# Attention row scores on 64 rows of the TensorE array, two heads at once, in bursts of four, with four PSUM banks instead of three

## What is computed

```python
q, k, v = (proj(Wq), proj(Wk), proj(Wv))            # 16 heads of 16
scores = jnp.einsum('bhsd,bhtd->bhst', q, k) * scale
scores = jnp.where(mask[None, None, :, :], -jnp.inf, scores)
attn = jax.nn.softmax(scores, axis=-1)
out = jnp.einsum('bhst,bhtd->bhsd', attn, v)        # then Wo, rms norm, modulation
x = x + ...                                          # then a top-2-of-8 expert block,
                                                     # a low-rank block and a quaternion block
```

## Time and profile before

| | |
|---|---|
| median of 3 runs | 1164.3 us (1163.31 to 1166.56) |
| span of the profiled execution | 1162.1 us |
| PE busy | 1122.4 us, 97% |
| DVE busy | 770.8 us, 66% |
| ACT busy | 803.1 us, 69% |
| POOL busy | 512.6 us, 44% |

### The profile page before, as it was taken

How to read it: one execution, slowest core, us unless ns; L and a number is a source line. 1 busy time by engine, 2 the same in 40 slices (tenths; PEclk the granted TensorE clock), 3 DMA queues, 4 the chain that set the end, 5 groups by cost and what they waited for, 6 DMA issues and landing times.

```text
span 1162.1 us, 23399 instructions
## 1 busy us (share of the span) xinstructions
PE 1122.4 (97%) x7520; PEld 763.4 (66%) x7520; DVE 770.8 (66%) x2265; ACT 803.1 (69%) x1752; POOL 512.6 (44%) x837
## 2 busy tenths in 40 slices
PE   8899999999999999998989999999999999999988
PEld 4333434434334343342418999998999999999968
DVE  4877777787887878878745434355555555667747
ACT  2578888787787877877786756655666666666645
POOL 8424135583755837657462365354222223222220
PEclk8999999999999999999999999999999999999999
DMA  8665638367384572843837488856566766723536
GB/s 220 193 195 189 219 100 250 124 215 231 119 257 138 198 235 94 242 157 133 286 101 269 115 309 306 267 120 133 155 193 190 213 193 179 226 48 70 164 91 217
DMA packets 101616, 213.64 MB, mean 184 GB/s; under 512 B 10917, under 2 KB 71341, under 8 KB 93046
## 3 DMA queue, kind: packets, MB, share of 16 engines
q1 hardware_dynamic: 86038, 192.42, 51.1%
q0 software_dynamic: 14304, 18.69, 9.0%
q10 hardware_dynamic: 1152, 1.05, 0.4%
HBM read 239.28 MB, written 74.29 MB: 270 GB/s over the span
## 4 chain that ended last, share of the span: by engine, by line
PE 46%; ACT 3%; issue 1%; DVE 1%; POOL 1%; DMA 1%; another core or an unknown queue 0%; ACTq 0%; POOLq 0%
PE bank L1084 38%; PE bank L1247 1%; PE bank L1189 1%; PE bank L1099 1%; ACT pt L1355 1%; PE bank L1170 1%; DMA x<-yout,rows 1%; PE bank L1113 1%; PE bank L1174 1%; PE bank L1207 1%; PE bank L1282 0%; PE bank L1155 0%; PE bank L1227 0%; ACT full L1433 0%
## 5 line engine op out<-in xcount | busy, mean ns | idle before, releaser
L1628 DVE CUSTOM_DVE_ANT_0 junk<-bank,mneg 128x512 bf16<-128x512 f32 x512 | 333.0, 683 | 119.0 <-PE bank L1155 116.3
L1355 ACT ACTIVATE pt<-bank 128x512 f32<-128x512 f32 x512 | 301.0, 594 | 67.8 <-PE bank L1170 29.7
L1975 POOL DMA_INDIRECT x<-yout,rows x78 | 122.8, 1574 | 292.9 <-ACT yout L1438 249.6
L1084 PE MATMUL bank<-hid,w 128*128 128x256 f32 x1872 | 242.7, 286 | 4.2 <-DVE hid L1776 3.8
L1084 PEld LDWEIGHTS bank<-hid,w 128*128 128x128 f32 x1872 | 229.3, 190 | 6.0 <-issue 4.8
L1776 DVE TENSOR_TENSOR hid<-full,hid 128x256 fp32r<-128x256 f32 x312 | 133.3, 431 | 135.3 <-ACT full L1433 126.8
L1428 ACT ACTIVATE hid<-bank,biases 128x256 fp32r<-128x256 f32 x312 | 149.4, 479 | 91.6 <-PE bank L1084 88.0
L1433 ACT ACTIVATE full<-bank,biases 128x256 f32<-128x256 f32 x312 | 148.7, 477 | 0.0
L1174 PE MATMUL bank<-mneg,identb 128*128 128x512 bf16 x386 | 146.9, 381 | 0.0
L1084 PE MATMUL bank<-rowsT,w 128*128 128x256 f32 x936 | 122.9, 284 | 0.9 <-issue 0.9
L1084 PE MATMUL bank<-w,hid 128*128 128x256 f32 x936 | 121.9, 283 | 1.5 <-DVE hid L1776 1.5
(11 more groups left out here) (184 smaller groups left out, 1445.2 us busy)
## 6 DMA issues: line engine op xcount, KB each, us to landing
w<-split_weights SPq DMA_DIRECT2D x80, 1024.0 KB
w<-split_weights SPq DMA_DIRECT2D x40, 2048.0 KB
split_weights<-w_parts SPq DMA_DIRECT2D x64, 512.0 KB, 3.8
w_parts<-in_W SPq DMA_DIRECT2D x64, 256.0 KB, 4.3
split_parts<-parts SPq DMA_DIRECT2D x28, 384.0 KB, 2.6
rows<-routed SPq DMA_DIRECT2D x39, 258.0 KB, 3.4
stacks<-split_parts SPq DMA_DIRECT2D x36, 256.0 KB, 5.2
qst<-split_parts SPq DMA_DIRECT2D x24, 256.0 KB, 5.3
```

Source lines behind the costliest of these rows:

```text
L1084: product = T.matmul(ps, w[p], x[q], start=(k == 0 and n == 0), stop=(k == len(weights) - 1 and n == 2))
L1355: A.activation(pt[n % len(pt)][:, :], bank[3 + n % 2][:, :], ACT.Exp, scale=float(D) ** -0.5).then_inc(exped.sem, 1)
L1628: V.tensor_tensor_reduce(junk[n % 2][:, :], bank[n % 3][:, :], mneg[:, 0, st, :], 1.0, FLOOR, ALU.add, ALU.max, rowmax[gi % 2][:, hh, st:s ...
L1975: G.indirect_dma_start(x2_dram, bass.IndirectOffsetOnAxis(ap=rows[j % NS][:, tt, E + 1:E + 2].bitcast(U32), axis=0), yout[j % NY][:, tt], ...
```

## The change

- The row scores take four pairs of parts (64 contraction rows) instead of six (96). The stacks are laid out anew: heads 0 and 1 of each group have these 64 rows at partitions 0 to 63, heads 2 and 3 at partitions 64 to 127. The products of a step's four rows are issued together, at the step's start, in the order heads 0, 2, 1, 3, so that neighbours lie on different halves of the array. DVE still reads them one by one.
- The rows have four banks (0, 1, 2, 7). As long as there are rows, all side work and `maxima_rows` use bank 6 alone. Steps of the chain that need it are put off until one of certain steps or two columns stand between them and the last user, and the places at which `todo` is worked off change.
- `weigh` comes after the second column of its step instead of the third; `maxima_rows` at the end of a group's first step instead of its second.
- The columns of heads 2 and 3 use all 128 rows (some of them zero), those of heads 0 and 1 the same 98.
- The stacks are filled by 24 transfers in a batch, of half the size, and the shift rows by two instead of one. POOL writes the constants of the shift as fp32 words and zeroes the unused rows.
- In the first two groups the rows go one by one: first heads 0 and 1 of both groups, then heads 2 and 3. The projections of the next batch come one step earlier.

```diff
+ROW_PAIRS = 4
+KR = ROW_PAIRS * D
+ROW_HEADS = (0, 2, 1, 3)
+ROW_BANKS = (0, 1, 2, 7)
...
-FIRST_PROJECTS = range(3, 7)
+FIRST_PROJECTS = range(2, 6)
...
+ONE_BANK = ("project", "project_v", "modulation", "maxima_rows", "project_o", "turn_x1", "gate", "place")
+APART = 2
...
+def slot_of(h):
+
+    g, hh = divmod(h, GH)
+    return hh // 2 * (H // 2) + g * (GH // 2) + hh % 2
+
+
+def pair_rows(half, r):
+
+    if r < ROW_PAIRS:
+        first, step = half * KR + r, ROW_PAIRS
+    else:
+        first, step = (KR, KR // 2)[half] + r - ROW_PAIRS, len(PAIRS) - ROW_PAIRS
+    return slice(first, first + (D - 1) * step + 1, step)
...
+def bank_free(order):
+
+    cols = 0
+    for step in reversed(order):
+        if step[0] in ONE_BANK:
+            return False
+        if step[0] in ("layer1", "layer2", "layer3"):
+            return True
+        cols += step[0] == "col"
+        if cols == APART:
+            return True
+    return True
...
+            if 2 <= i < GROUPS:
+                out.append(("rows", i, k))
             for n in range(GH):
-                if i < GROUPS:
-                    out.append(("row", i, n, k))
-                if k == 0 and n == 0 and 0 <= i - 1 < GROUPS:
+                if i < 2:
+                    found = first_rows[(i * ST + k) * GH + n]
+                    out.extend((("one_row", *found), ("row", *found)))
+                elif i < GROUPS:
+                    out.append(("row", i, ROW_HEADS[n], k))
...
-                if n == 2 and k % 2 == 0 and 0 <= g < GROUPS:
+                if n == 1 and k % 2 == 0 and 0 <= g < GROUPS:
                     out.append(("weigh", g, kt))
                     out.append(("weigh", g, kt + 1))
...
+                if n == 1 and k % 2 and i >= 2 and todo and todo[0][0] != "project" and bank_read(out.order):
+                    work_off()
...
-            for _ in range(2 if len(todo) > 12 else 1):
-                if todo and i >= 2:
-                    work_off()
+            if todo and i >= 2 and (k or i > GROUPS) and bank_read(out.order):
+                work_off()
...
+        home = 6 if row_steps[0] < turn_place[s] < row_steps[-1] else 6 + n % 2
...
                     for r in range(n, len(PAIRS), STACK_STEPS):
-                        start((qst, kst)[qk][b % 2][r:KQ:len(PAIRS), :, :].rearrange("d (a h) s -> d a (h s)", a=2),
-                              split_dram[b, qk, PAIRS[r][qk]].rearrange("(a d h) s -> d a (h s)", a=2, d=D)).then_inc(dma_stack[qk], 16)
+                        for half in range(2):
+                            start((qst, kst)[qk][b % 2][pair_rows(half, r), half * (H // 2):(half + 1) * (H // 2), :],
+                                  split_dram[b, qk, PAIRS[r][qk]][half * P:(half + 1) * P, :].rearrange("(d h) s -> d h s", d=D)
+                                  ).then_inc(dma_stack[qk], 16)
...
+        def row_product(gi, hh, st):
+            b, half, at_slot = gi // NG, hh // 2, slot_of(gi % NG * GH + hh)
+            n = row_place[gi, hh, st]
+            if n >= len(ROW_BANKS):
+                pe.wait_ge(*max_found.at(rows_at[n - len(ROW_BANKS)]))
+            elif ROW_BANKS[n] == 7:
+                pe.wait_ge(*evicted(before_rows_user))
+            stacks_loaded(pe, b, half)
+            rows = slice(half * KR, (half + 1) * KR)
+            T.matmul(bank[ROW_BANKS[n % len(ROW_BANKS)]][:, :], qst[b % 2][rows, at_slot, st * P:(st + 1) * P],
+                     kst[b % 2][rows, at_slot, :], start=True, stop=True).then_inc(row_scored.sem, 1)
...
+        def shift_constants(i):
+
+            halves = [slice(half * (H // 2), (half + 1) * (H // 2)) for half in range(2)]
+            for stacks in (kst, qst):
+                constant(G.memset, stacks[i][0:KR // 2, halves[1], :].bitcast(F32), 0.0)
+            for half in range(2):
+                constant(G.memset, kst[i][shift_rows_of(half), halves[half], :].bitcast(F32), TWO_MINUS_ONES)
```

More of the change, by code:

```diff
@@ L1 @@
+import struct
 import numpy as np
@@ L123, in wait_ge, with shift_rows_of, bank_read, chain @@
             self.engine.wait_ge(sem, value)
-def chain(b, out):
+def slot_of(h):
[7 more added lines that the diff above has]
+    return slice(first, first + (D - 1) * step + 1, step)
+def shift_rows_of(half):
+    return slice(0, SHIFTS) if half else slice(KQ, KQ + SHIFTS)
+def bank_free(order):
[9 more added lines that the diff above has]
+    return True
+def bank_read(order):
+    last = next(step[0] for step in reversed(order) if step[0] in ONE_BANK + ("logits", "ranks"))
+    return last not in ("gate", "place")
+def chain(b, out, attention=False):
+    def bank():
+        while attention and not bank_free(out.order):
+            yield
     apart = 2 if b == B - 1 else 1
@@ L148, in chain @@
         yield
+        yield from bank()
         out.append(("turn_x1", b, k))
@@ L265, in work_off @@
         if step[0] == "chain":
-            chains.append(chain(step[1], out))
+            chains.append(chain(step[1], out, True))
         else:
@@ L270, in work_off @@
                 rests.append(("rest",) + step[1:])
-        if todo and todo[0][0] == "stack":
+        if todo and todo[0][0] in ("stack", "chain"):
             work_off()
@@ L287, in attention_order @@
     out.extend(value_steps(0))
+    first_rows = [(i, hh, st) for n in range(2) for i in range(2) for st in range(ST) for hh in (2 * n, 2 * n + 1)]
     for i in range(GROUPS + 3):
@@ L771, in misc_bank @@
     def misc_bank(step):
-        n = misc_place[step]
-        return bank[6 + n % 2], n >= 2 and evicted(misc_users[n - 2])
+        home, user = misc_home[step]
+        if home == 7 and user == before_rows_user and turn_place[step] > row_steps[-1]:
+            return bank[home], max_found.at(rows_at[-1])
+        return bank[home], user and evicted(user)
     def value_bank(b, st):
@@ L1147, in tensor_program @@
                 T.matmul(ps[0:B, :], condS[:, :], wc, start=True, stop=True).then_inc(modulated.sem, 1)
-            elif name == "row":
-                gi, hh, st = at
-                b, h = gi // NG, gi % NG * GH + hh
-                n = row_place[gi, hh, st]
-                if n >= 3:
-                    pe.wait_ge(*max_found.at(rows_at[n - 3]))
-                stacks_loaded(pe, b, h // (H // 2))
-                T.matmul(bank[n % 3][:, :], qst[b % 2][0:KQ, h, st * P:(st + 1) * P], kst[b % 2][0:KQ, h, :],
-                         start=True, stop=True).then_inc(row_scored.sem, 1)
+            elif name == "one_row":
+                row_product(*at)
+            elif name == "rows":
+                gi, st = at
+                for hh in ROW_HEADS:
+                    row_product(gi, hh, st)
             elif name == "col":
                 gi, kt, hh = at
-                b, h = gi // NG, gi % NG * GH + hh
+                b, at_slot = gi // NG, slot_of(gi % NG * GH + hh)
+                stack = slice(0, P) if hh // 2 else slice(0, KQ + SHIFTS)
                 n = col_place[gi, kt, hh]
```

45 lines of the change are left out of this document (29 added, 16 removed).

## The result

| | before | after |
|---|---|---|
| median | 1163.9 us (1163.31 to 1166.56, 4 runs) | 1217.0 us (1210.06 to 1218.56, 4 runs) |
| span of the profiled execution | 1162.1 us | 1215.6 us |
| mean granted clock | 0.996 | 0.972 |

The changed kernel is slower by the factor 1.044 (1.0413 to 1.0472), 53 us. The forecast was 1182 with a range up to 1200. The direction was right, the size was not, and the time lies outside the range.

A forecast was written before the change was run, and what follows sets the result against it. PE's issue was taken as the bound, ACT close behind. Batches 12.7, squares 4, columns only 1.5 and start 0.5 gave 18.7 us, less some 1 for DVE: span 1180, median 1182; forecast 1170 to 1200, range 1146 to 1200.

The forecast's parts named there:

- Removed work: In 120 steps (groups 2 to 31) four rows of 0.876 us become a burst of 0.66, saving 0.22 a step.
- rival C: Row bursts: the halves don't overlap, a burst takes 1.10 us; plus 38 us, 1220; chance 0.04.
- B: Row bursts: no edges, 0.44 us, waits as computed; no change in time, 1164; chance 0.12.
- Waits for ACT: Columns and seeds in a batch's eight pairs: new waits for ACT sum to 7.3 us a batch.
- the squares: Eight squares a batch on ACT, now mostly in its idle time: 0 to 4 us a batch, 0.5 taken, plus 4.
- DVE at the last rows: Where DVE is late with the fourth bank, four products and columns behind wait: 0 taken, up to 5 us in all.
- The start: First two groups stay at DVE's rhythm; POOL's constants delay the first low parts and rows: 0.5 us.
- Rival D: Bank 6: each of 20 users a batch waits for its reader; 4 us a batch more, 1212; chance 0.05.
- POOL's constants: Shift constants as four of 2048 words: no change from 6.92 us, or up to 1.5 for the steps between.
- Columns only: Two groups without rows: the weighing's shift costs about 0.4 us in each of four pairs, plus 1.5.

The follow-up runs named there:

- moved projection: Changed kernel with the projection behind the second transpose put one step later, ahead of the gate's step: 1194.1 us, ratio 1.0252 to the kernel before.
- other seeds: Changed kernel with seeded columns at heads 2 and 3 of weighing steps, instead of head 3, then head 0: 1179.8 us, ratio 1.0146 to the kernel before.
- row order: Changed kernel with each burst's rows in the order heads 0, 1, 2, 3 instead of 0, 2, 1, 3: 1217.9 us, ratio 1.0435 to the kernel before.
- spread: Changed kernel with batch 1's first projections at steps 2, 4 and 7, the fourth later, instead of 2 to 5: 1214.0 us, ratio 1.0426 to the kernel before.
- doubled start: Changed kernel with each row product of the first two groups issued twice: 1220.2 us, ratio 1.049 to the kernel before.

## Why the prediction was wrong

- **Removed work: right.** A burst of 0.66 us forecast, 0.63 measured; rival C (no overlap) fell, and B (no edges) too.
- **Waits for ACT: right in kind, one place too small.** Content without rows' saving (6.30 us), side work and waits of the prediction give, in the order of the batch, 11.4, 9.5, 9.0, 8.1, 9.0, 8.1, 9.6 and 10.2 us for the eight pairs, 75 in all. Measured: 11.55, 10.46, 9.46, 8.10, 9.05, 8.07, 9.87, 10.42, sum 76.98. The pair with the gate is 1.0 short: I put its waits at 1.3 and the squares at 0.5 for a whole batch, "mostly in its idle time", but a low part and a square stand before the exponential that the second column needs. The projection behind the second transpose waited 0.77 us where I had 1.2. The pair without side work, forecast at 7.6, took 7.63 and, where ACT had a low part in between, 8.14.
- **The clock: missing.** The failed step is that the sum went at full clock. The earlier trace rows show 1.00 for a PE that is busy 396 of 400 us, and I added 7 us of waits a batch without asking what the clock does then. Where they gather, around the gate, the clock falls to 0.50. Four dips in the steady part at 3 to 5 us each give 17, a fifth at the last rows some 2.0. With 19 us it is the largest term that has no place in the sum. The moved projection and the other seeds, which take the dips between 208 and 550 us away, give back 23 and 37 us, waits and clock together.
- **DVE at the last rows: 0 taken, 3.6 measured.** The prediction had the term ("four products and the columns behind them wait; I take 0, up to 5 us in all"), and in that one burst it came.
- **The start: 0.5 us forecast, 8.9 measured.** The step that failed was "the first two groups stay at DVE's rhythm". Rival D had the right mechanism (a bank waits for DVE's rest behind row maxima), and I priced it in the batches, where PE has no wait for a rest at all, and not in the start, where it costs some 7 us together with the clock (7.5 in the kernel before with one bank). POOL's constants were right: in the changed kernel's timeline the four take 7.36 us, against 6.92.
- **Columns only: 1.5 forecast.** From the first weighing behind the last burst to the first expert product it is 31.26 us instead of 27.21 (from 636.58 and 586.89). Of the 4.1 us more, 1.8 are the last weighing, which now stands ahead of that product and not behind it, so 2.2 are left.
- **Sum.** Start 8.4 at the sixth weighing, five batches at 3.3 a batch without their dips 16.4, their dips 12.4, and 16.6 from there on, of which a dip 4.9 and the last rows 5.9. Forecast were 2.2 a batch with the squares, 1.5 for columns only, 0.5 at the start, and nothing for the dips.
- The range ended at 1200 because D was priced at 1 us a place and C at 38, and no rival joined waits and clock. "PE busy 97% at clock 1.00" was read as a bound, and not as the condition of that clock.

## What to carry over

When work of a full engine is made shorter and its operations are gathered, look at what they stood between: here each row product covered a wait for ACT. Price the clock as a term of its own wherever waits of a microsecond gather on a PE that was busy without a break, and put the longest side work there, not before. A bank that several users share is dear where a queue between them (DVE's rest behind row maxima) is the pace, so look for it in the start, not only in the steady part. And compare pairs that hold the same work: a pair of 8.1 us with a projection in it says nothing of one without.

## What the runs showed of the hardware

- A dip of the clock lasts longer than the waits ahead of it: 0.57, 1.04 and 0.20 us of waits were followed by some 10 us at 0.50, and the dip cost 4.75 us beside them.
- Such waits didn't always bring it: in the changed kernel one batch of five stayed at 1.0, and over the four kernels with this gate pair unaltered (changed, row order, spread and doubled start) 15 of 20 had a dip. In two of three kernels with doubled row products the clock fell to 0.50 at about 20 us, with products back to back, in the third not.
- Four products of 64 rows take 0.54 us with halves alternating and 0.54 with neighbours on the same half, and 0.09 us more before the first.
